# A fused attention and product-key FFN kernel: transposed scores first in the slots of the last attention step, searches spread over the first FFN tile, and a last tile that ends in parts

## The reference

```
x = x + proj(softmax(mask(q @ k.T / sqrt(8))) @ v)        # q, k, v of layernorm(x)
xl = layernorm(x); xn = batchnorm(xl)
sim = (xn @ w_q.T).keys            # 8 heads, 2 halves, 32 values each
s, i = top_k(sim, 8)               # per half
scores, pk = top_k(s_x + s_y, 8)   # 8 of the 64 pairs
o = gelu(xl . key_in[idx]) * softmax(scores)
x = x + sum(o * key_out[idx])      # 1024 experts
```

## Time and profile before

| what | us |
|---|---|
| median of 3 runs | 1659.61 |
| lowest and highest run | 1656.77 and 1664.16 |
| the profiled execution's own time | 1659.77 |
| its span, first to last instruction | 1658.0 |
| attention's last instruction but DMAs (DVE, 692.15 + 0.69) | 692.84 |
| first product of the FFN that counts (L1104) starts | 697.59 |
| DVE busy | 1484.1 |
| PE busy | 1470.9 |
| ACT busy | 1313.8 |
| POOL busy | 1270.5 |

### The profile page before, as it was taken

How to read it: one execution, slowest core, us unless ns; L and a number is a source line. 1 busy time by engine, 2 the same in 40 slices (tenths; PEclk the granted TensorE clock), 3 DMA queues, 4 the chain that set the end, 5 groups by cost and what they waited for, 6 DMA issues and landing times.

```text
span 1658.0 us, 33309 instructions
## 1 busy us (share of the span) xinstructions
PE 1470.9 (89%) x10762; PEld 1021.1 (62%) x10762; DVE 1484.1 (90%) x4616; ACT 1313.8 (79%) x1805; POOL 1270.5 (77%) x1547
## 2 busy tenths in 40 slices
PE   5899999999999998788888888888888888888887
PEld 3445555555555554366767767677676766667666
DVE  4889999999999995389999999999999999999997
ACT  1266766766667666589999999999999999999995
POOL 1155556556565556399999999999999999999992
PEclk9799999999999999889999999999999999999999
DMA  6444545544455541100000000000000000000000
GB/s 155 90 96 100 122 116 113 114 110 108 116 121 115 113 104 36 58 1 20 1 20 20 1 20 20 9 13 20 20 1 20 20 2 20 20 17 4 14 7 8
DMA packets 73630, 86.40 MB, mean 52 GB/s; under 512 B 9872, under 2 KB 63760, under 8 KB 68752
## 3 DMA queue, kind: packets, MB, share of 16 engines
q1 hardware_dynamic: 72840, 82.70, 21.0%
q10 hardware_dynamic: 616, 1.57, 0.6%
HBM read 58.30 MB, written 25.95 MB: 51 GB/s over the span
## 4 chain that ended last, share of the span: by engine, by line
POOL 17%; ACT 14%; DVE 11%; issue 8%; PE 8%; DMA 0%; DVEq 0%; ACTq 0%; SPq 0%
POOL SUM L864 17%; DVE W L1094 7%; ACT E L987 6%; PE WT L1161 5%; ACT L904 2%; ACT L903 2%; PE MB L1104 1%; ACT W L947 1%; PE MB L1107 1%; DVE SMALL L1040 1%; ACT SIM L897 1%; DVE M8Y L1023 1%; ACT GE L903 0%; ACT GE L908 0%; ACT GE_first L903 0%
## 5 line engine op out<-in xcount | busy, mean ns | idle before, releaser
L864 POOL TENSOR_TENSOR SUM<-SIM 128x1024 f32<-128x1024 f32 x480 | 899.7, 1918 | 31.2 <-DVE W L1094 27.2
L1161 PEld LDWEIGHTS WT<-idf,W 128*128 128x128 f32 x4096 | 478.6, 147 | 212.0 <-issue 128.4
L1094 DVE SCALAR_TENSOR_TENSOR W<-SUM,SMALL,E 128x1024 f32<-128x1024 f32 x448 | 560.7, 1280 | 43.2 <-ACT E L987 42.8
L1161 PE MATMUL WT<-idf,W 128*128 128x128 f32 x4096 | 544.6, 284 | 57.3 <-DVE CT L1074 38.0
L280 POOL TENSOR_SCALAR_AFFINE_SELECT PT<-PT 128x128 f32<-128x128 f32 (+1 forms) x1024 | 335.5, 353 | 249.2 <-ACT PT L391 213.3
L987 ACT ACTIVATE E<-SUM,NB 128x1024 f32<-128x1024 f32 x448 | 495.4, 1116 | 20.5 <-DVE W L1094 17.8
L450 DVE CUSTOM_DVE_ANT_0 SY<-SY,bandf 128x384 f32<-128x384 f32 x512 | 273.5, 574 | 0.0
L391 ACT ACTIVATE PT<-TX 128x512 f32<-128x512 f32 x256 | 152.9, 597 | 113.8 <-PE TX L586 113.7
L471 DVE TENSOR_REDUCE mx<-SX 128x2 f32<-128x512 f32 x256 | 174.5, 682 | 40.2 <-PE SX L568 37.8
L393 ACT ACTIVATE PT<-TY 128x768 f32<-128x768 f32 x256 | 207.5, 811 | 2.3
L614 PE MATMUL PV<-PT,V 128*32 128x384 f32 (+1 forms) x2048 | 164.2, 438 | 0.9 <-POOL PT L280 0.7
(11 more groups left out here) (135 smaller groups left out, 1910.0 us busy)
## 6 DMA issues: line engine op xcount, KB each, us to landing
Q<-q_parts SPq DMA_DIRECT2D x288, 64.0 KB
K<-k_parts SPq DMA_DIRECT2D x90, 192.0 KB
q_parts<-qp SPq DMA_DIRECT2D x16, 384.0 KB, 2.4
k_parts<-kp SPq DMA_DIRECT2D x15, 384.0 KB, 2.4
xin<-in_x SPq DMA_DIRECT2D x16, 256.0 KB, 3.0
xres<-in_x SPq DMA_DIRECT2D x16, 256.0 KB, 9.6
x<-X SPq DMA_DIRECT2D x16, 256.0 KB, 2.3
x2T<-X2T SPq DMA_DIRECT2D x16, 256.0 KB, 2.1
```

The source lines that it names most:

```text
L864: return eng.tensor_tensor(SUM[(q * FH + h) % RING][:, :].rearrange("p (i j) -> p i j", i=NK), sx, sy, ALU.add)
L1094: nc.vector.scalar_tensor_tensor(out=W[h % WRING][:, :], in0=SUM[(k * FH + h) % RING][:, :], scalar=TOP[q][:, h, TOPK - 1:TOPK], in1=E[(n ...
L1161: o = pe.matmul(WT[:, e, :], W[h % WRING][:, e * P:(e + 1) * P], ident[:, :], is_transpose=True, start=(h == 0 and e % 4 == 0), stop=(h == ...
```

## The change

- In step 16, from slot 2 on, PE issues `scoresT` at the head of the slot, ahead of the slot's other products. ACT's program is the same.
- `keep_clock` after the last attention step issues 9 products, not 6.
- In tile 0 of the FFN, parts 0 and 1 of the next tile's search run ahead of slot 0's mask and parts 2 and 3 ahead of slot 2's; the rest stays in slot 4.
- The last tile's product WT times GE is made in two halves, with a semaphore each, and PE starts on the first half. ACT's `finish` of tile 62 leaves slot 5 of tile 63 and comes after all exponentials. The last group's store is two DMAs, tiles 0 to 2 and tile 3.

```diff
@@ attention, tensor, step @@
+                turned_first = c == SEQS and h >= 2
+                if turned_first:
+                    scoresT(t, c, h)
...
-                if 0 <= c - 1 < SEQS:
+                if 0 <= c - 1 < SEQS and not turned_first:
                     scoresT(t, c, h)
 
         steps(pe, step)
-        keep_clock(6)
+        keep_clock(9)
@@ tables @@
 EVEN_PARTS = ((), (), (), (), ((1, 0), (1, 1), (1, 2), (1, 3), (1, 4), (1, 5), (1, 8), (2, 0), (2, 1), (1, 9)), (), ((1, 6),), ((1, 7),))
+FIRST_PARTS = (((1, 0), (1, 1)), (), ((1, 2), (1, 3)), (), ((1, 4), (1, 5), (1, 8), (2, 0), (2, 1), (1, 9)), (), ((1, 6),), ((1, 7),))
@@ ffn, sync @@
         steps(sp, group)
-        store(GROUPS - 1, 1)
+        for tiles, done in ((slice(0, GT - 1), GT - 1), (slice(GT - 1, GT), GT)):
+            await_(sp, S["out_copied"], (GROUPS - 1) * GT + done)
+            sp.dma_start(outg[GROUPS - 1][:, tiles, :], OUT[1][:, tiles, :]).then_inc(S["out_stored"], 16)
+        await_(sp, S["out_stored"], (GROUPS + 1) * 16)
@@ ffn, scalar, group @@
-                    if h == COPY_OUT and (real or k):
+                    if h == COPY_OUT and (real or k) and (more or k < GT - 1):
                         finish(j - 1, *((g, b, k - 1) if k else (g - 1, 1 - b, GT - 1)))
...
         steps(act, group)
+        finish(GROUPS * GT - 2, GROUPS - 1, 1, GT - 2)
         finish(GROUPS * GT - 1, GROUPS - 1, 1, GT - 1)
@@ ffn, vector, group @@
-                    for ahead, part in (ODD_PARTS if k % 2 else EVEN_PARTS)[h]:
+                    for ahead, part in (ODD_PARTS if k % 2 else EVEN_PARTS if real else FIRST_PARTS)[h]:
...
         steps(dve, group)
-        experts(GROUPS * GT - 1, GROUPS - 1, 1, GT - 1)
+        dve.wait_ge(S["weights_turned"], GROUPS * GT * FH)
+        dve.wait_ge(S["gelu_ready"], GROUPS * 2)
+        dve.wait_ge(S["out_product"], GROUPS * GT - 2)
+        for half, to in ((0, "half_weighted"), (1, "experts_weighted")):
+            es = slice(half * BLK // 2, (half + 1) * BLK // 2)
+            nc.vector.tensor_tensor(CT[1][:, es, :], WT[:, es, :], GE[1][:, es, (GT - 1) * P:GT * P], ALU.mult).then_inc(S[to], 1)
@@ ffn, tensor, outputs @@
-            pe.wait_ge(S["experts_weighted"], j + 1)
+            last = j == GROUPS * GT - 1
+            if last:
+                pe.wait_ge(S["half_weighted"], 1)
+            else:
+                pe.wait_ge(S["experts_weighted"], j + 1)
             for e in range(BLK):
+                if last and e == BLK // 2:
+                    pe.wait_ge(S["experts_weighted"], j + 1)
                 o = pe.matmul(po, CT[k % 2][:, e, :], key_out[:, e, :], start=False, stop=(e == BLK - 1))
```

More of the change, by code:

```diff
@@ L796, in ffn @@
              "out_stored ranked candidates top_ready top_less_max top_exp exp_sum log_sum bias_ready "
-             "l_x_moved l_sums l_shifted l_weights").split()
+             "half_weighted l_x_moved l_sums l_shifted l_weights").split()
     S = {n: sem("f_" + n) for n in names}
```

## The result

| | before | after |
|---|---|---|
| median over all runs (17 each, same chips) | 1656.56 | 1663.46 |
| lowest and highest run | 1653.81, 1664.16 | 1659.26, 1667.2 |
| the profiled execution's own time | 1659.77 | 1665.17 |
| its span | 1658.0 | 1663.4 |

The ratio is 1.003 (95%: 1.0019 to 1.0042), some 5 us slower and within the 0.5% band. The runs of the changed kernel stand in two groups, 8 of them from 1659.3 to 1660.8 and 9 from 1663.5 to 1667.2; so the two medians lie 6.9 us apart. The forecast had the place and the sign of each part; it took the first part 4 us too small.

A forecast was written before the change was run, and what follows sets the result against it. No single engine was taken as the bound; the circle of ACT, DVE and PE sets the pace. From 1659.77, +5.5 (order), -2.0 (searches) and -1.85 (end) gave 1661.4, less 0.16 for the median: 1661.3 us, range 1654 to 1667.

The forecast's parts named there:

- the first part: Step 16's new PE order: +5.5 us including a share for the clock, with ends of 3.5 and 7.5.
- the four places named: Timeline places where waits matter: the FFN's chain through POOL's sums, attention step 16, the first FFN tile, tile 63.
- +4.8: Step 16's tail: last values start near 681.9 instead of 677.13 at full rate, delaying the whole FFN by 4.8 us.
- The last L391 starts near 679: Sign for step 16: ACT's last exponential, in slot 15, starts near 679, against 674.85 before.
- +1.5 us. I take half of it: Slots 11 to 13 of step 16: half-rate PE would double values and transposes, +1.5 us; half was counted.
- rival 3: Step 16, slots 12 to 15: PE falls to half rate and stays there, 9 us more, about 1670; chance 0.03.
- my case: Whole kernel: the main forecast of 1661.3 us, with ends 1656.4 and 1664.5; chance 0.76.
- cost nothing: End of the attention block: three more keep_clock products of about 0.14 us cost nothing; possible gain up to 1.0, taken as 0.
- -2.0: First FFN tile: spread searches save 2.0 us, between 1.6 and 2.4, capped by POOL's 19th sum in tile 2.
- -1.0: Tile 63: without the copy ahead of the last exponentials, CT comes at 1650.6 against 1651.71, a gain of 1.0 us.
- -0.55: Last tile: halving CT lets PE start after half of 1.23 us, saving 0.55 (0.5 to 0.6).
- 0.3: Kernel end: last store of 64 KB, not 256, saves 0.3 us (0 to 0.7).

The follow-up runs named there:

- experiment 6: Kernel before plus the new step 16 order, with useless PE filler products between TX and TY and after slots 1 to 4, 6, 8, 10, 11, 12; ratio 1.0016.
- experiment 4: Kernel before plus the new step 16 order, with ACT's copies of U, X2T and AT moved behind their slot's exponentials; ratio 1.0013.
- experiment 5: Kernel before plus the new order only in slots 5 to 10 of step 16, which hold no ACT copies; ratio 1.0.
- experiment 1: Kernel before plus the new step 16 order alone (keep_clock(6), old search tables and last tile); median 1669.67 us, ratio 1.007.
- experiment 3: Kernel before plus the new step 16 order, with useless PE filler products after slots 2, 3, 4, 6, 8, 10, 11, 12; ratio 1.003.
- 7: Kernel before, old order, with step 16's values of slots 1, 5, 7, 9, 13, 15 halved and the second half behind TY; ratio 0.9991.
- 9: Kernel before plus only the spread searches of the first FFN tile; ratio 0.9998.
- 2: Changed kernel with the old order in step 16, everything else of the change kept; ratio 0.9991.
- 8: Changed kernel with the old step 16 order and the values of slots 1, 5, 7, 9, 13, 15 halved around TY; median 1652.34 us, ratio 0.9962.
- 11: Changed kernel, old step 16 order, values of slots 1, 5, 7, 9, 13 halved, three fillers after slots 1, 2, 4, 6, 8, 10; ratio 0.9977.

## Why the prediction was right, and where it was too small

- **Bound and places.** Right: PE's busy total rose by 9.4 us, no other engine's moved by 1 us, and the ledger closes with the four places named. CT of tile 0 to CT of tile 62 differs by 0.4 us in 914.
- **The order, "+4.8" at full rate.** Right in mechanism and nearly in size: experiment 6 measured 4.84 with its fillers, some 4.4 without them, experiment 4 took the mechanism away, experiment 5 showed that the other slots are neutral. The waits are ahead of U (twice), X2T and AT. The two parts were less exact than the sum: the steps put the last exponential 4.0 us late and add 0.8 at the tail; less the 0.4 of the fillers the runs show some 3.4 and 1.1 (the last values follow the last exponential by 3.34 in the changed kernel and in experiments 1 and 3, before by 2.28). "The last L391 starts near 679" missed (683.96): 0.6 us of it is from ahead of step 16, and with no stretch at half rate it stood at 32.73 from the copy of V (experiment 6), which is 679.0 here.
- **The clock's share of this term, "+1.5 us. I take half of it".** This step was mis-sized. It measured some +5.1 in the profile (9.55 - 4.4), +1.2 in experiment 3 and +2.5 in experiment 1. I looked for the fall in slots 11 to 13, where PE is busy least, and one of 6.8 us came there, behind a stretch with PE busy 1.57 of 3.4 us; the longer stretch came at slot 3, ran 10.2 us, and took the values from 1.28 to 2.36 us and all other products with them. It is the mechanism of rival 3 in a milder form: rival 3 asked for 9 us more than my case, and 4 came. In the trace the longest idle time of PE in the stretch ahead of the fall in slot 3 is 0.36 us, so no long gap was needed. The Trainium skill (TensorE: Matmul & The Clock Gate, "Why this matters for your kernels") asks to avoid long gaps between bursts; here keeping to that was not enough. Another section of that page of the Trainium skill ("A second HAM failure mode: psum-queue depth-cycling") tells of a kernel whose clock went up and down as PE idled briefly and often between groups of products. This trace looks like that, and it is the section that the prediction should have weighed.
- **Whether the order makes the fall likelier** stays open. The four profiles with the whole order and light or no filling all have a stretch in step 16 (after, 1, 3, 4), and so has the one with the order in six slots (5); of five with neither the order nor fillers two have (7 and 9; not before, 2 and 8). These are too few to put a rate on it.
- **keep_clock(9), "cost nothing".** Right: 51.91 and 51.92.
- **The searches, "-2.0" capped at 2.4.** Right: 2.31 at the cap, where ACT waits 0.40 for POOL's sum. The third mask waited 0.52, a hair above the 0.5 that was named. How much of it is the searches and how much the clock is not shown. With a second stretch of 6.8 us at half rate in the first tile the old table takes 27.5 to 27.9 us to CT (before, 1, 5, 7), with one of 3.4 us 26.3 to 26.6 (3, 4, 6); the new table takes 25.0 to 25.2 with one of 3.4, or 24.2 without, and never had one of 6.8. The stretch before it varies too, 13.7 or 17.1 us. With the shorter stretch the activation in tile 2 comes after 39.2 to 39.5 with the old table and 38.4 with the new, so there the searches are worth about 1 us; whether they also cause the shorter stretch stays open.
- **The end, "-1.0", "-0.55", "0.3".** Measured -1.09, -0.54 and -0.76. Only the store was under-sized, just above its 0 to 0.7.
- **Sum.** 5.5 - 2.0 - 1.85 = +1.6 forecast; with the order at full rate the parts are 4.4 - 2.3 - 2.4 = -0.3, with the clock of this execution +4.8, and 0.6 came from ahead of step 16. The ratio says +5.0 (3.1 to 6.9). All of it lies within 0.5% and the time within the range; +0.1% was forecast and +0.3% came, and without the falls it would have been about none. That 1661.3 is only 2.2 us from the measured median is in part luck: it counts from a base of 1659.6, the median of three runs, where 17 runs give 1656.56. From that base the same sum gives 1658.2, 5.3 us too low.
- **The spread of the runs.** Part of it is made long before the change. ACT's copy of V of the second sequence in the kernel before (the first is at 74.22):

```profile
109.55 0.59 ACT L327 COPY V<-MB 128x512 f32<-128x512 f32 x1 [1.13 <-PE MB L645]
```

The same in the changed kernel (the first is at 72.63):

```profile
111.94 0.59 ACT L327 COPY V<-MB 128x512 f32<-128x512 f32 x1 [0.58 <-PE MB L648]
```

The step takes 35.3 us in the one and 39.3 in the other, with PE at half rate from 54.8 on for 20.5 us and from 54.7 on for 30.7. In the 13 profiles of this study, alike up to there, it takes 34.5 to 35.3 us (before, 3, 6, 7, 9, 11) or 39.2 to 39.6 (the others), and the copy of V in step 16 starts anywhere from 640.5 to 648.4. Such differences ahead of the change may be why pieces of 1 to 2 us that the traces show don't show in the times, and why the runs fall into groups; it wasn't tried.

## What to carry to other kernels

Before moving a product behind another on PE, ask which copy on another engine waits for it and what is queued behind that copy: here four copies ahead of exponentials cost some 3.4 us at full rate and the early products behind TY 1.1 more, and with the copies moved behind the last exponential was 1 us late instead of 6, with as much time at half rate. To start a product early, split the one ahead of it, so that no dependent copy moves: with the rest of the change that was 0.4% faster here, by itself (in a profile with 10.2 us at half rate) too little to measure. Where PE does small products with short waits in between, give every order that adds waits a price for half rate that covers the whole step, not only its emptiest slots.

## What the hardware showed that was not expected

- PE's granted clock fell to 0.50 right behind stretches in which PE was busy 2.22, 2.49 and 2.10 of 3.4 us (after, 7, 9), with no idle time longer than 0.36, 0.56 and 0.56 us in them; in the kernel before (first row) and in experiment 2 (second), the stretches below led to no fall. With the same instructions of step 16 the clock fell in one execution (9) and not in others (before, 2); so it was with 7 and 8.

```profile
653.00:656.40 3.40, 2.49 (x23) 0.84 (x22) 0.00 (x0) 2.07 (x4) 2.35 (x8) 1.00 0.01 2
```

```profile
653.00:656.40 3.40, 2.25 (x22) 0.78 (x23) 0.00 (x0) 2.36 (x4) 2.57 (x8) 1.00 0.03 10
```

- Each microsecond at half rate cost step 16 some 0.3 to 0.4 us: in the new order (the changed kernel and experiments 1 and 3, over the estimate of 4.4 at full rate), in the old (9 against before, 4.85 for 13.7) and in the split one (7 against 8, 4.01 for 10.2). Only experiment 5 has less, 0.5 for 3.4.
- With PE busy 9.60 of 10 us by fillers it stayed at 1.00, but in the old order fillers cost 1.2 us themselves.
